# Selecting attention with a folded search, selection on the pool engine, chunks of 128 columns and another order of the projections

## What is computed

```python
q = x @ Wq;  k, v = split(x @ Wkv)          # 16 heads of 64
k = concat([mem_k, k]); v = concat([mem_v, v])   # 16 memory slots ahead of the 512 tokens
dots = einsum('bhid,bhjd->bhij', q, k) * scale
dots = einsum('bhij,hk->bkij', dots, pre_proj)   # the heads are mixed
dots = where(causal mask, dots, -max)
top = top_k(dots, 64)                            # per row
dots = where(dots < top[..., -1], -max, dots)    # keep the 64 largest of a row
out  = softmax(dots) @ v;   y = out @ Wout + bout
```

## Time and profile before

| | us |
|---|---|
| median of 3 runs | 5798.12 |
| the profiled execution: its own time | 5793.93 |
| its span in the profile | 5792.2 |
| selecting attention's search, first `MAX8` to last selection | 2338.8 to 3968.9 |
| DVE busy over the whole span | 4467.9 |
| PE busy over the whole span | 4949.5 |
| POOL busy over the whole span | 2310.7 |

### The profile page before, as it was taken

One profiled execution on the slowest core, in us unless ns is written; L12 is line 12 of the kernel. 1 busy time (PEld: TensorE's weight loads), 2 busy tenths in 40 slices (PEclk: granted clock), 3 DMA queues, 4 the chain that ended last, 5 costly groups with the idle time before them and its releaser, 6 DMA issues. The chain is left out here.

```text
span 5792.2 us, 137900 instructions
## 1 busy us (share of the span) xinstructions
PE 4949.5 (85%) x53334; PEld 3142.3 (54%) x53334; DVE 4467.9 (77%) x8591; ACT 3358.8 (58%) x7305; POOL 2310.7 (40%) x3182
## 2 busy tenths in 40 slices
PE   4775999999999996667677677675999999999997
PEld 1332666666666664334334344343666666666665
DVE  5996777777777774898998998995777777777775
ACT  2432777777777774334334333332677777777775
POOL 1222666666666662000000000000666666666663
PEclk7997999999999998877777787776999999999999
DMA  0000222222222221000000000000222222222221
GB/s 17 0 0 27 73 74 66 77 65 74 64 78 67 74 63 38 2 1 2 1 1 2 1 2 1 1 2 22 72 71 70 74 68 74 64 74 66 78 65 38
DMA packets 162493, 247.30 MB, mean 43 GB/s; under 512 B 36228, under 2 KB 56640, under 8 KB 161734
## 3 DMA queue, kind: packets, MB, share of 16 engines
q1 hardware_dynamic: 161862, 238.65, 15.8%
HBM read 36.15 MB, written 1.05 MB: 6 GB/s over the span
## 5 line engine op out<-in xcount | busy, mean ns | idle before, releaser
L940 POOL TENSOR_TENSOR f_rope<-f_rope,f_t 128x1024 f32<-128x1024 f32 x384 | 906.4, 2360 | 522.2 <-DVE f_t L854 522.2
L953 POOL TENSOR_TENSOR f_rope<-f_rope,f_rn 128x1024 f32<-128x1024 f32 x384 | 731.2, 1904 | 57.1 <-POOL f_rn L932 3.0
L490 PE MATMUL psum<-f_wqkv,f_xs 128*128 128x512 f32 x1536 | 731.4, 599 | 23.0 <-DVE f_t L854 23.0
L859 DVE TENSOR_REDUCE f_ss<-f_sq 128x16 f32<-128x1024 f32 x384 | 459.7, 1197 | 338.3 <-ACT f_sq L721 335.9
L1733 DVE MAX8 tk_m<-tk_work 128x8 f32<-128x408 f32 (+28 forms) x1624 | 679.7, 461 | 0.0
L1772 POOL TENSOR_TENSOR X<-tk_y,X 128x128 f32<-128x128 f32 x16 | 7.0, 436 | 1663.2 <-ACT tk_y L1678 1663.2
L1738 DVE MATCH_REPLACE8 tk_work<-tk_m,tk_work 128x408 f32<-128x408 f32 (+28 forms) x1392 | 624.9, 458 | 0.0
L684 ACT ACTIVATE f_kT<-psum 64x512 f32<-64x512 f32 (+1 forms) x960 | 485.5, 525 | 84.4 <-PE psum L481 74.5
L721 ACT ACTIVATE f_sq<-psum 128x1024 f32<-128x1024 f32 x384 | 393.5, 1025 | 218.7 <-PE psum L490 218.4
L854 DVE TENSOR_TENSOR f_t<-psum,f_rot 128x1024 f32<-128x1024 f32 x384 | 466.0, 1214 | 0.0
L850 DVE TENSOR_TENSOR f_rope<-psum,f_rot 128x1024 f32<-128x1024 f32 x384 | 465.2, 1212 | 0.0
(11 more groups left out here) (237 smaller groups left out, 10080.9 us busy)
## 6 DMA issues: line engine op xcount, KB each, us to landing
f_v<-f_v_tok SPq DMA_DIRECT2D x1152, 128.0 KB, 2.4
f_v<-f_v_tok SPq DMA_DIRECT2D x768, 64.0 KB, 2.0
f_wqkv<-in_Wqkv SPq DMA_DIRECT2D x36, 512.0 KB, 4.0
f_wo<-in_Wo SPq DMA_DIRECT2D x12, 512.0 KB, 4.3
f_w<-in_W SPq DMA_DIRECT2D x12, 341.0 KB, 3.2
f_w<-in_W SPq DMA_DIRECT2D x24, 64.0 KB
tk_wkv<-in_Wkv SPq DMA_DIRECT2D x1, 1024.0 KB
out<-y_tok SPq DMA_DIRECT2D x4, 256.0 KB, 2.5
```

Of the source, the lines that this page charges most:

```text
L490: last = pe.matmul(psum[:, n, :], xs[:, j % 2, :], wqkv[:, INNER * which + 512 * n:INNER * which + 512 * (n + 1)], start=True, stop=True)
L859: dve.tensor_reduce(ss[:, H * half:H * (half + 1)], sq[:, half, :, :], AX_X, ALU.add).then_inc(s[f"{name}_ss"], 1)
L940: pool.tensor_tensor(part, part, t2[:, half, :, :], ALU.add).then_inc(s[f"{name}_added"], 1)
L953: pool.tensor_tensor(part, part, rn[:, H * half:H * (half + 1)].unsqueeze(2).to_broadcast([P, H, DH]), ALU.mult).then_inc(s[f"{name}_norme ...
```

## The change

- **Folded search.** A new `fold` writes, for a row of n columns with halves of h = n/2, the elementwise maximum of the two halves to `work[0:h]` and the minimum to `work[h:n]`. Rounds 0 to 3 search and overwrite only the h maxima, rounds 4 to 7 all n columns of `work`. (The i-th largest maximum has at most i - 1 other maxima and i - 1 minima above it, so the first 32 maxima are among the 64 largest.) `fold(p+1)` stands behind round 6 of pair p. `work` gets two buffers, `scores` three, `e` two.
- **Selection on POOL.** The DVE instruction L1753 goes. POOL's `select` makes a 0/1 mask from `scores` by comparing with the 64th value and multiplies `e` by it, two instructions for each unit. `copy_scores(p)` waits for `p_done` of pair p-3, and the last round of pair p for `p_done` of pair p-1.
- **Two pairs ahead.** PE and ACT do `raw_dots`, `mix` and their copies for pair s+2 in slot s, and `turn` for pair s-2. `weigh`, `turn_output`, `normalise`, `copy_output` are in even slots, `recip` behind round 4 of odd ones, one slot after its `weigh`.
- **Chunks of 128 columns.** `e` is cut at multiples of 128 from its column 0, memory included; `v` gets the memory values as its first 16 rows (by a matmul with the identity). A unit has one chunk less than before, except in the last block of a tile, where it has as many.
- **Projections** of q and k for later tiles go to parts 0 and 1, of v to part 3, `output` to part 5.

The core of the diff:

```diff
+                def fold(p):
+                    for j in range(2):
+                        unit = 2 * p + j
+                        n, h = extent(unit)[0], half(unit)
+                        dst, src = work[:, p % 2, j, :], scores[:, p % 3, j, :]
+                        dve.wait_ge(s["copied"], 1 + unit + 1)
+                        dve.tensor_tensor(dst[:, 0:h], src[:, 0:h], src[:, h:n], ALU.max).then_inc(s["folded"], 1)
+                        dve.tensor_tensor(dst[:, h:n], src[:, 0:h], src[:, h:n], ALU.min).then_inc(s["folded"], 1)
...
-                        src = [work[:, j, 0:cols[j]] if r else scores[:, parity, j, 0:cols[j]] for j in range(2)]
+                            src = [work[:, parity, j, 0:half(2 * p + j) if r < ROUNDS // 2 else cols[j]] for j in range(2)]
...
+                            if r == ROUNDS - 1 and selected(2 * p - 1):
+                                dve.wait_ge(s["p_done"], 1 + selected(2 * p - 1))
...
-                        if r == 5:
+                        if r == 4:
                             between()
+                        if r == 6:
+                            fold(p + 1)
...
-                            dve.scalar_tensor_tensor(e[:, j, 0:cols[j]], scores[:, parity, j, 0:cols[j]], m8[:, j, TOPK - 1:TOPK], e[:, j, 0:cols[j]],
-                                                     ALU.is_ge, ALU.mult).then_inc(s["p_done"], 1)
...
+                def select(unit):
+                    pool.wait_ge(s["e_done"], 1 + unit + 1)
+                    pool.wait_ge(s["kth"], 1 + selected(unit))
+                    pool.tensor_scalar(kept, kept, m8[:, j, TOPK - 1:TOPK], None, ALU.is_ge).then_inc(s["kept"], 1)
+                    pool.wait_ge(s["kept"], 1 + selected(unit))
+                    pool.tensor_tensor(probs, kept, probs, ALU.mult).then_inc(s["p_done"], 1)
...
+                    if pair >= 3 and selects(2 * pair - 6):
+                        act.wait_ge(s["p_done"], 1 + selected(2 * pair - 5))
...
-                    if slot + 1 < SLOTS:
-                        raw_dots(slot + 1)
-                    if 0 <= slot - 1 < SLOTS:
-                        turn(slot - 1)
+                    if slot + 2 < SLOTS:
+                        raw_dots(slot + 2)
+                    if 0 <= slot - 2 < SLOTS:
+                        turn(slot - 2)
```

More of the change, by code:

```diff
@@ L1330, in selected, with chunks, half @@
         return per_batch * b + sum(selects(x) for x in range(rest + 1))
+    def chunks(unit):
+        return divmod(extent(unit)[1], P)
+    def half(unit):
+        return extent(unit)[0] // 2
     def parts(c0, c1):
@@ L1517, in turn @@
                         unit = 2 * pair + j
-                        b, t, u = place(unit)
-                        wide = extent(unit)[1]
-                        m = wide - MEM - P * t
+                        full, rest = chunks(unit)
                         if selects(unit):
@@ L1638, in copy_scores @@
                         for lo, hi in parts(0, extent(unit)[1]):
-                            last = copy(scores[:, pair % 2, j, lo:hi], psum[:, MIXED + j if lo == 0 else RAW + j, 0:hi - lo])
+                            last = copy(scores[:, pair % 3, j, lo:hi], psum[:, MIXED + j if lo == 0 else RAW + j, 0:hi - lo])
                         last.then_inc(s["copied"], 1)
@@ L1650, in copy_turned @@
                         unit = 2 * pair + j
-                        b, t, u = place(unit)
-                        m = extent(unit)[1] - MEM - P * t
+                        full, rest = chunks(unit)
                         blk = unit // 4
@@ new lines, in _ @@
+                for i in range(CHUNKS):
+                    copy_v(0, i)
+                for slot in range(SLOTS + TAIL):
+                    T, part = divmod(slot, TILE_PAIRS)
+                    if slot + 2 < SLOTS:
+                        copy_raw(slot + 2)
+                    if slot % 2 == 0 and 0 <= (slot - 6) // 2 < SLOTS // 2:
+                        normalise((slot - 6) // 2)
+                    if 0 <= slot - 2 < SLOTS:
+                        copy_turned(slot - 2)
+                    if slot % 2 == 0 and 0 <= (slot - 6) // 2 < SLOTS // 2:
+                        copy_output((slot - 6) // 2)
@@ L1705, in _ @@
-                    if part == 5 and T + 1 < B * TILES:
-                        copy_q(T + 1)
-                    if slot % 2 == 1 and 0 <= (slot - 3) // 2 < SLOTS // 2:
-                        normalise((slot - 3) // 2)
+                    if slot + 2 < SLOTS:
+                        copy_scores(slot + 2)
+                    if part == 0 and T + 1 < B * TILES:
+                        copy_q(T + 1)
+                    if part == 1 and keys_due(T):
+                        copy_k(*keys_due(T))
@@ L1710, in _ @@
+                    if part == 3:
+                        for b, i in values_due(T):
+                            copy_v(b, i)
+                    if part == 5 and T >= 1:
+                        copy_y(T - 1)
             @block.vector
@@ L1772, in _ @@
                     pool.tensor_tensor(xt, y[:, :], xt, ALU.add).then_inc(s["added"], 1)
+                for slot in range(SLOTS + TAIL):
+                    if slot % TILE_PAIRS == 6 and slot >= TILE_PAIRS:
+                        add_y(slot // TILE_PAIRS - 1)
+                    for unit in (2 * slot - 2, 2 * slot - 1):
+                        if 0 <= unit < 2 * SLOTS and selects(unit):
+                            select(unit)
 def build(nc, a, out):
```

199 lines of the change are left out of this document (99 added, 100 removed).

## The result

The changed kernel takes 5533.31 us (median of 4 runs, 5526.95 to 5547.09), the one before 5797.19 in the same job: ratio 0.9548, 95% interval 0.9532 to 0.9564. That is inside the range, and 28 us above the forecast of 5505. The profiled executions are 5530.04 and 5793.93 us: 263.9 us less, where the sum had 289.

What follows compares the result with a forecast made beforehand. DVE was taken to bound three tiles of each batch, the PE and ACT chain the fourth. 268 + 44 + 5 - 20 - 7 - 1 = 289 us less than 5793.93 gave 5505 us, range 5455 to 5595.

Steps and rivals of the forecast that it cites:

- The fold and the selection: DVE in tiles 3 to 1: half-width rounds 0 to 3 save 67.0 us a batch, folds and removed selection cancel; 268 us.
- The lock: DVE's small `tensor_scalar` of the tops stands for POOL's product at the shared port: 20 us lost, 0.17 a pair.
- "whole price" rival: Each DVE top waits for a whole POOL product, 94 us in place of 20: 5579 us, chance 0.15.
- Tile 0, 44 + 5 us: PE's extra pair of head start and shorter slots save 11 us a batch, 44; the last tile 5 more.
- Start: Phase start: DVE's tops of pair 1 wait for the first exponentials, 7 us more, once.
- End: Phase end: POOL's last two selections take 1 us more than DVE's.
- POOL's pace: Selection on POOL makes nobody wait by pace: 0 us, at 4.2 us a pair of tile 3 beside DVE's 14.9.
- PE and ACT as a bound: Rival: PE and ACT's slot chain becomes the bound, with 1 us more a slot: 5586 us, chance 0.14.

Runs made afterwards that it cites:

- experiments 1 and 2: Changed kernel with the negation of the tops on ACT (1: 5471.51 us), or on DVE as two 128x1 instructions instead of one 128x2 (2: 5496.02 us).
- experiment 7: Changed kernel with the projections of q and k back in the sixth and fifth slot of a tile, as in the kernel before: 5567.27 us.
- experiment 8: Changed kernel with search rounds 4 to 6 left out, so the threshold is wrong and everything else runs: 5252.34 us (2 runs).
- experiment 3: Changed kernel with DVE's negation of the tops ahead of the first round's two replacements rather than behind them: 5516.28 us.

## Why the prediction was nearly right

The profiled 263.9 us come from the trace as follows, against the sum's terms.

**The fold and the selection, 268 us: right.** Tiles 3 to 1 save 233.4 us in four batches (the first wait left out); with the 43.2 us of stands in them 277. Without stands a tile takes 118.3, 92.6 and 66.7 us, 0.5 to 0.9 less than predicted. The four fold instructions of a pair of 984 columns take 1.29 us, from 2765.19 to 2766.48 in the trace, where the sum had 1.28 for 952.

**The lock, 20 us: the step that failed.** The mechanism was the one named, with the right instruction; only its size was wrong: 45.5 us, 43 of them beside the product. The prediction let the first product end 1.98 us after POOL's start and the top fall 1.85 after it, a stand of 0.1 to 0.2. In the timeline above the top comes 1.70 after it, but the product only *begins* at 1.54 and ends at 2.72, so that it is met whole. The comparison was priced at 0.81 us, with the product's 1.17 as the upper end, and takes 1.46 at 472 columns, beyond both; the rest follows. In tiles 1 the negation comes just before the product starts or just after, and in most pairs has no stand. The "whole price" rival (94 us) had nearly the right picture of tiles 3 and 2 and the wrong one of the others; experiments 1 and 2 show that no other DVE instruction stands for POOL by an amount that matters.

**Tile 0, 44 + 5 us: 44.8, in part by luck.** 9.0, 14.6 and 14.8 us in the first three batches, where the step had 11, and 6.5 in the last, where it had 16: the kernel before took only 52.95 us there, not 63.1. The places of the projections carry them: with the old places (experiment 7) the first three tiles take 63 to 66 us again, with PE's head start and the shorter slots still in, which are what the step counted. What the step also missed is that this tile's length is PE's busy time and some 10 us (48.63 = 38.47 + 10.16 above), and that busy time goes with the granted clock. Stretches of 4 us in the first batch's tile 0, the columns as in the earlier trace rows:

```profile
2652.00:2656.00 4.00, 2.80 (x47) 2.24 (x47) 0.00 (x0) 2.36 (x10) 0.00 (x0) 1.00 0.02 4
2656.00:2660.00 4.00, 4.00 (x105) 2.70 (x108) 2.56 (x25) 1.08 (x5) 0.00 (x0) 0.71 0.00 0
2660.00:2664.00 4.00, 3.55 (x40) 2.54 (x38) 3.16 (x27) 1.72 (x7) 0.50 (x2) 0.50 0.02 6
2664.00:2668.00 4.00, 3.31 (x5) 1.01 (x5) 3.91 (x35) 0.86 (x2) 1.11 (x3) 0.50 0.00 2
...
2672.00:2676.00 4.00, 3.36 (x74) 2.54 (x74) 2.02 (x20) 2.47 (x11) 1.76 (x4) 1.00 0.01 4
```

PE, busy for the whole of a stretch at 2656, falls from 2.4 to 1.2 GHz there and is back at 2.4 in the stretch at 2672; the tile takes 54.1 us. In the second batch's tile 0 it keeps 2.4 GHz from 2989 on, and the tile takes 48.6:

```profile
2989.00:2993.00 4.00, 2.65 (x48) 2.06 (x37) 0.03 (x1) 3.24 (x14) 0.00 (x0) 1.00 0.01 2
...
3009.00:3013.00 4.00, 2.82 (x70) 2.42 (x73) 2.69 (x26) 2.67 (x13) 1.37 (x3) 1.00 0.01 2
```

**Start, 7 us: 6.9.** DVE's second negation waited 6.91 us for the first exponentials, at 2365.82. **End, 1 us: 3.3**: the last maxima are 19.5 us ahead of the next phase's first matmul, where they were 16.2. In every kernel run here with the new order and the whole search it is 19.2 to 19.5, with the selection on DVE too; so POOL is not the cause, the order is: one more block's weighing stands there between.

**What no term had:** the phase's first search starts 5.4 us later, 4.3 of them because the memset ahead of it starts at 2310.68 instead of 2306.33. In thirteen profiled kernels that memset starts between 2305.1 and 2313.3, whatever was changed after it; and what follows the phase took 1.3 us less. In sum, 233.4 + 44.8 - 6.9 - 3.3 - 5.4 + 1.3 = 263.9. Of the 25 us that the sum had too many, 23 are the stands of tiles 3 to 1, 6 the late start and the end, 4 tile 0, and the fold gave 9 back.

**POOL's pace, 0 us: right**, if at 5.5 us a pair in tile 3 (from 2767.30 to 2772.78), not 4.2. DVE waited for a selection once, 2.04 us, in the last tile. PE and ACT as a bound (5586 us) is out by experiment 8.

## What to carry to other kernels

An instruction moved to an idle engine can still cost the busy one the time for which a shared port is held: find the busy engine's instructions that can meet it, place them on one time line with the moved one's real durations, and let them run where they can't meet (another engine, or a shape that doesn't take the port; here 62 and 37 us). What such a meeting costs is decided by tenths of a microsecond of phase, so a faster instruction ahead of it can make it worse, as the fold did. Where an engine that sets the pace stops and starts, part of its length is its granted clock, and small changes elsewhere move it by 5 to 12 us in 50.

## What the runs showed of the hardware

- A POOL comparison of fp32 by a per-row value is dearer than a product of two tensors: 1.46 us for 1.18 at 472 columns, 0.94 for 0.75 at 264. From 264 to 528 columns (0.94 to 1.60 us) it costs 2.5 ns a column.
- A DVE `tensor_scalar` of 128x2 that begins more than 0.02 us after POOL's product stands for it to its end, 1.1 us at most; one of 128x1 stood in none of 256 cases. The Trainium skill, "SBUF — State Buffer", section "Who interferes with whom", has the lock held for the whole instruction. The product agrees with it; the comparison does not: met with 0.69 us of 1.58 to go it let the negation through, met with 0.40 of 1.46 it held it, and experiment 3's 109 meetings part at 0.53 to 0.56 of its length (in experiment 8 one at 0.60 was let through). Why is open.
- `MAX8` and the replacement were not slowed by POOL: in after, none of the 1,099 that can be compared took over 0.02 us more beside it than its shape does alone, and DVE's tiles without stands came out 0.5 to 0.9 us under the sum from the kernel before.
- In tiles 0 of the first three batches, the same work of PE took 48.0 to 59.8 us, with the granted clock between 0.97 and 0.70, among kernels that differ in the negation's form and place and the first exponentials only. What sets the phase in which the clock falls was not settled.
